# The tail of a scan-and-attention kernel: other engines spread and multiply the last reciprocals, and the last scales, shifts and sums change their order

## The chip, the core and the metric

The kernel runs on one core of a Trainium2 chip. The metric is the device time of one execution in microseconds (us). Engines are named as in the profile: PE is TensorE, DVE is VectorE, ACT is ScalarE, POOL is GpSimd and SP is SyncE.

## What is computed

The input is eight images of 64 channels, 64 x 64. Four directional scans go over them first (each row becomes itself plus relu of a 9-tap convolution of the row before it); the change does not touch them. Then comes linear attention, with four heads of 32 channels, between two group norms:

```python
xn = group_norm(x, gn1_w, gn1_b)
q, k, v = split(conv1x1(xn, w_qkv))            # heads of 32 channels, 4096 positions
q = elu(q) + 1; k = elu(k) + 1
k_sum = k.sum(positions); kv = k^T v           # per head
out = (q @ kv) / (q @ k_sum + 1e-6)
out = group_norm(conv1x1(out, w_out), gn2_w, gn2_b) + x
```

## The kernel before

After the scans the images are in `cols_w`. The attention takes them one after another, b = 0 to 7 (B = 8), through `iteration(b, par, cur, prev, pp)`, which every engine has in a version of its own. Iteration b computes keys, values and queries of image b (`cur`), the denominators, their reciprocals and the first outputs of image b-1 (`prev`), and the second group norm of image b-2 (`pp`). Each engine goes through its own instructions in the order in which they are written; semaphores join the engines.

An image is 4 chunks of 512 columns (128 partitions: two halves of 64 channels). The queries of an image are 8 units of 128 x 512 in `qp`, two to a chunk. To divide by the denominators:

- PE sums them (`denominators`, L586), DVE takes the reciprocals (L901), 128 x 128 for each half m of the units (units 0 to 3, 4 to 7).
- `broadcast(c, m)` on SP writes them to HBM (L320) and reads them back spread over the partitions of a head (L326) into `recip_b`.
- POOL multiplies four units (`normalise_units`, L395) and PE projects two units to one chunk of output (`output`, L597), which ACT copies to SBUF (`collect`, L1142).
- The second group norm: statistics of four chunks on DVE (L912), their aggregate (L906), two matmuls with one column (`group_sums`, L560) with small DVE operations between them, then on POOL a power, a product and a shift (`scale_and_shift`: L399, L403, L407), on ACT scale and shift (`affine`, L1177), on POOL the sum with the scanned image (L424), and SP's stores (L333).

After iteration 7 each engine has a tail, written out by hand. There are two images in it: the last but one (6), of which half is still to be multiplied and projected, and the last (7). In the tail:

- DVE L994/L995 masks the sums of image 7, PE `last_denominators` (L647) gives its denominators for m = 0 and 1, DVE `last_reciprocal` (L982, L986) the reciprocals.
- PE `reciprocals_back(m)` (L659) spreads them into four PSUM banks `back_ps` by 32 small matmuls, with no DMA. DVE `last_normalised(u)` (L990) multiplies a unit by such a bank. Units 4 to 7 use banks that units 0 to 2 must have left (`normed_last`).
- PE `one_before_last(i)` (L666) projects chunks 2 and 3 of image 6, from units that POOL has multiplied, and `last_output(i)` (L673) the chunks of image 7. DVE takes their statistics from PSUM (L1016), ACT copies them out (L1189).
- `group_sums` (L560) comes twice for image 6 (DVE `deviation(5)`, `variance(6)`, L964 to L973) and twice for image 7 (`deviation(7)`, `variance(8)`).
- POOL: `scale_and_shift` of image 6, three quarters of its sum with the scanned image (`residual(q)`, L436), `scale_and_shift` of image 7, the fourth quarter.
- Image 7 is done in two halves of its rows. First half: DVE L1027 (product with the scale, plus the scanned image), then ACT L1200 adds the shift. Second half: ACT L1197 scales and shifts, DVE L1032 adds the scanned image.
- Each half of an image leaves in two stores of 256 KB, one for each half of the partitions. SP issues all four of image 6 and then two of image 7, in this order; ACT issues the other two of image 7 (L1205).

## Time and profile before

| | us |
|---|---|
| median of 3 runs | 705.79 |
| lowest and highest of the 3 | 705.42 and 707.0 |
| the profiled execution | 706.54 |
| span of its trace | 704.7 |
| mean granted TensorE clock | 0.974 |
| PE, DVE, ACT, POOL busy | 636.4, 570.4, 462.6, 140.8 |

The span is measured from the first to the last event of the trace; the profiled execution took 1.8 us more than its span. The scans take about the first 450 us, the eight images the rest, some 27 us each. The tail that the change rewrites is the stretch from about 664 us to the end. A view in order of time gives a start, a duration, the engine, the line and what was written from what; a group of n instructions has xn. Brackets give the idle time before it and what ended it.

### The profile page before, as it was taken

The numbers are of one execution on the slowest core, as the hardware profiler recorded it, in microseconds if no ns is written. First come the engines' busy times: TensorE is split into PE (matmuls) and PEld (weight loads), VectorE is DVE, ScalarE is ACT, GpSimd is POOL, SyncE is SP. The second block draws the span as 40 slices with busy tenths as digits, with TensorE's granted clock in tenths as the row PEclk, the third lists the DMA queues.
The fourth block names the chain that finished last, engine by engine and source line by source line (L and its number), as shares of the span: only waits on it lengthen the run. The fifth ranks groups of instructions, "written<-read, shape, count | busy, mean of one in ns | idle before, by whom it ended". The sixth has DMA issues, their size and how long they took to land.

```text
span 704.7 us, 27312 instructions
## 1 busy us (share of the span) xinstructions
PE 636.4 (90%) x10484; PEld 538.4 (76%) x10484; DVE 570.4 (81%) x1943; ACT 462.6 (66%) x1061; POOL 140.8 (20%) x115
## 2 busy tenths in 40 slices
PE   4999999999999899999999999698888898898960
PEld 4899999898888899999999999556454464554530
DVE  4899998888888798989999999897595686785682
ACT  3555666999999666666666666574666676676531
POOL 0023000000000000000000000000627658549363
PEclk9999999999999999999999999889999999999995
DMA  9999850000000000000000000002342835835756
GB/s 175 203 201 198 166 108 1 1 0 0 0 0 0 1 2 0 0 0 0 1 1 0 0 0 0 0 2 60 71 106 57 171 85 104 178 74 122 159 87 120
DMA packets 63611, 43.27 MB, mean 61 GB/s; under 512 B 42000, under 2 KB 56144, under 8 KB 63568
## 3 DMA queue, kind: packets, MB, share of 16 engines
q1 hardware_dynamic: 60272, 41.89, 30.1%
q10 hardware_dynamic: 3296, 0.82, 0.6%
q8 instruction: 26, 0.43, 0.3%
q14 instruction: 17, 0.14, 0.1%
HBM read 33.39 MB, written 9.31 MB: 61 GB/s over the span
## 4 chain that ended last, share of the span: by engine, by line
DVE 31%; PE 26%; issue 17%; POOL 12%; ACT 7%; DMA 3%; DVEq 1%; ACTq 1%; POOLq 0%; SPq 0%
PE bank L468 20%; DVE scan_rows L735 9%; POOL rows_h L395 9%; DVE parts L721 8%; DVE parts L735 7%; DVE fin L794 3%; ACT cols_w L1077 3%; POOL fin L424 2%; DMA rows_h<-bounce 2%; ACT parts L1061 2%; DVEq L735 1%; PE bank L597 1%; DMA yn<-L_conv_k_td 1%; PE bank L518 1%; PE bank L544 1%
## 5 line engine op out<-in xcount | busy, mean ns | idle before, releaser
L468 PE MATMUL bank<-parts 128*128 128x124 f16 (+2 forms) x7560 | 433.5, 219 | 16.1 <-DVE parts L236 8.7
L468 PEld LDWEIGHTS bank<-parts 128*128 128x128 f16 x7560 | 417.7, 98 | 31.8 <-issue 12.0
L1061 ACT ACTIVATE parts<-parts 128x128 f16<-128x128 f16 x508 | 157.1, 309 | 125.9 <-DVE parts L735 104.3
L721 DVE TENSOR_TENSOR parts<-scan_rows,parts 128x128 f16<-128x128 f32 x508 | 149.4, 294 | 14.2
L735 DVE SCALAR_TENSOR_TENSOR parts<-bank,cols_w 128x128 f16<-128x128 f32 x378 | 109.5, 290 | 19.9 <-PE bank L468 4.7
L735 DVE SCALAR_TENSOR_TENSOR scan_rows<-bank,cols_w 128x128 f32<-128x128 f32 x378 | 105.7, 280 | 0.1
L395 POOL TENSOR_TENSOR rows_h<-rows_h 128x512 f32<-128x512 f32 x56 | 81.9, 1495 | 73.4 <-DMA rows_h<-bounce 73.4
L384 POOL TENSOR_TENSOR scale<-dev,half 128x2 f32<-128x2 f32 (+1 forms) x2 | 2.1, 1038 | 412.0 <-DVE dev L819 412.0
L1077 ACT ACTIVATE cols_w<-scan_rows 64x256 f32 (+1 forms) x128 | 82.7, 646 | 2.3
L861 DVE SCALAR_TENSOR_TENSOR kp<-ex,bank 128x512 f32<-128x512 f32 x64 | 40.8, 679 | 43.4 <-ACT ex L1155 42.4
L1069 ACT ACTIVATE cols_w<-scan_rows 128x256 f32 x126 | 52.5, 417 | 5.7 <-DVE scan_rows L735 0.3
L1163 ACT ACTIVATE ex<-bank,minus_one 128x512 f32<-128x512 f32 x64 | 40.5, 688 | 17.2 <-PE bank L530 16.7
L1155 ACT ACTIVATE ex<-bank,minus_one 128x512 f32<-128x512 f32 x64 | 40.6, 689 | 13.0 <-PE bank L518 13.0
L735 DVE SCALAR_TENSOR_TENSOR parts<-bank,rows_h 128x128 f16<-128x128 f32 x126 | 36.7, 291 | 15.3 <-PE bank L468 7.9
L871 DVE SCALAR_TENSOR_TENSOR rows_h<-ex,bank 128x512 f32<-128x512 f32 x64 | 40.9, 679 | 5.2 <-ACT ex L1163 5.2
L544 PEld LDWEIGHTS bank<-kp,tok 128*64 128x64 f32 x512 | 28.7, 139 | 13.9 <-issue 10.5
L544 PE MATMUL bank<-kp,tok 128*64 128x128 f32 x512 | 35.7, 282 | 1.6 <-DVE kp L861 1.6
L597 PE MATMUL bank<-rows_h,mix 128*64 128x512 f32 x104 | 28.0, 615 | 8.8 <-POOL rows_h L395 8.6
L735 DVE SCALAR_TENSOR_TENSOR scan_rows<-bank,rows_h 128x128 f32<-128x128 f32 x126 | 35.2, 280 | 0.0
L1128 ACT ACTIVATE tok<-bank 128x512 f32<-128x512 f32 x32 | 19.2, 599 | 15.8 <-PE bank L504 15.7
L794 DVE BATCH_NORM_STATS2 fin<-cols_w x96 | 28.7, 299 | 0.0
L1142 ACT ACTIVATE rows_h<-bank 128x512 f32<-128x512 f32 x26 | 15.7, 605 | 19.5 <-PE bank L597 19.4
(133 smaller groups left out, 549.2 us busy)
## 6 DMA issues: line engine op xcount, KB each, us to landing
rows_h<-bounce SPq DMA_DIRECT2D x56, 256.0 KB, 5.0
cols_w<-x SPq DMA_DIRECT2D x12, 896.0 KB, 13.8
out<-fin SPq DMA_DIRECT2D x12, 512.0 KB, 7.7
cols_w<-x SPq DMA_DIRECT2D x6, 640.0 KB, 10.8
cols_w<-x SPq DMA_DIRECT2D x6, 256.0 KB, 7.2
out<-rows_h SPq DMA_DIRECT2D x6, 256.0 KB, 4.7
bounce<-recip SPq DMA_DIRECT2D x14, 64.0 KB, 3.3
out<-rows_h ACTq DMA_DIRECT2D x2, 256.0 KB, 6.5
```

Of the source, the lines that this page charges most:

```text
L395: nc.gpsimd.tensor_tensor(qp[:, 1 - par, u, :], qp[:, 1 - par, u, :], recip_b[:, u, :], ALU.mult).then_inc(normed, 1)
L468: last = nc.tensor.matmul(conv_rows[g][u % SLOTS][:, :, to], w[:, k, d, :], rows_16[:, u % SLOTS, g * GB:(g + 1) * GB, of], start=part_n = ...
L544: nc.tensor.matmul(acc_ps[d * C:(d + 1) * C, 0:P], tok[:, i % 2, n * P + d * C:n * P + (d + 1) * C], kp[:, (2 * i + d) % 4, n * P:(n + 1) ...
L721: nc.vector.tensor_tensor(low[:, slot, gb, :], state[:, slot, gb, :], high[:, slot, gb, :], ALU.subtract).then_inc(low_ready[g], 1)
L735: nc.vector.scalar_tensor_tensor(out=to, in0=conv[g][u % SLOTS][:, 0:GB * J].rearrange("p (b j) -> p b j", b=GB), scalar=0.0, in1=add, op0 ...
L794: nc.vector.bn_stats(stats[:, b, bass.ds(n * 2 + (g - 2), 1), :].rearrange("p o s -> p (o s)"), cols[:, bass.ds(n * -BODY + (W + first), c ...
L861: nc.vector.scalar_tensor_tensor(out=kp[:, m % 4, :], in0=ex[:, m % 2, :], scalar=1.0, in1=key_ps[m % 2][:, :], op0=ALU.min, op1=ALU.max)\
L871: nc.vector.scalar_tensor_tensor(out=qp[:, par, u, :], in0=ex[:, 2 + u % 2, :], scalar=1.0, in1=query_ps[u % 2][:, :], op0=ALU.min, op1=AL ...
L1061: act.activation(high_down[:, slot, gb, :], high[:, slot, gb, :], ACT.Copy, scale=1.0 / LOW_SCALE).then_inc(down_ready[g], 1)
L1069: act.activation(to, state[:, slot, :, :], ACT.Copy).then_inc(saved, 1)
L1077: s = act.activation(dst, state[pw * C:(pw + 1) * C, (u + 1) % SLOTS, :, :], ACT.Copy)
L1155: act.activation(ex[:, m % 2, :], key_ps[m % 2][:, :], ACT.Exp, bias=minus_one[:, :])\
```

## The change

Image 6, the last but one: its second half of reciprocals no longer goes through HBM (`broadcast(B - 2, 1)` and POOL's `normalise_units` are left out in iteration 7). PE spreads them with `reciprocals_back(B - 2, 1, back_before_ps)`, and DVE multiplies units 4 to 7 of image 6 (`normalised_before_last`). The projection of its chunk 1 moves from iteration 7 to the tail.

Image 7, the last: DVE multiplies units 0 to 5. ACT copies the spread reciprocals of units 6 and 7 to `recip_b`, and POOL multiplies them (new semaphores `back_copied`, `normed_late`). The outputs come in the order 0, 1, 3, 2.

The end: POOL computes the scale of image 7 after one quarter of image 6's sum instead of three; its shift is computed by DVE; ACT does image 6's `affine` after two of the four copies of image 7; DVE's last sum no longer waits for ACT's last step.

```diff
+LAST_ORDER = (0, 1, 3, 2)
...
+        back_before_ps = (key_ps[0], key_ps[1], tok_ps, query_ps[0])
...
@@ SyncE @@
-            for m in range(2):
-                broadcast(B - 2, m)
+            broadcast(B - 2, 0)
...
             for h, rows in enumerate(HALVES):
-                sp.wait_ge(last_ready, h + 1)
+                sp.wait_ge(last_ready[h], 1)
                 store(B - 1, rows, fin_tail[:, 1], (0,))
@@ GpSimd @@
-                if prev:
+                if prev and has_next(b, cur):
                     normalise_units(b, par, 1)
...
+            for u in (6, 7):
+                pool.wait_ge(back_copied, u - 5)
+                nc.gpsimd.tensor_tensor(qp[:, 1, u, :], qp[:, 1, u, :], recip_b[:, u, :], ALU.mult)\
+                    .then_inc(normed_late, 1)
             pool.wait_ge(tail_read, 6)
             scale_and_shift(B, 0)
-            for q in range(3):
+            residual(0)
+            pool.wait_ge(tail_read, 8)
+            scale_of_output(B + 1, 1)
+            for q in (1, 2, 3):
                 residual(q)
-            pool.wait_ge(tail_read, 8)
-            scale_and_shift(B + 1, 1)
-            residual(3)
@@ TensorE @@
-                    if i == 3 and prev:
+                    if i == 3 and prev and has_next(b, cur):
...
                         output(b - 1, 1 - par, 1)
...
+            pe.wait_ge(back_loaded, 16)
+            pe.wait_ge(kp_ready, KBANKS * B)
+            pe.wait_ge(tok_ready, 4 * B)
+            pe.wait_ge(qp_ready, UNITS * B - 1)
+            reciprocals_back(B - 2, 1, back_before_ps)
+            pe.wait_ge(acc_read, B)
+            pe.wait_ge(qp_ready, UNITS * B)
+            sums(query_ps[1]).then_inc(tail_done, 1)
             pe.wait_ge(small_read, small_step(B - 1, 5))
+            pe.wait_ge(normed, UNITS * (B - 2) + 4)
+            one_before_last(1)
+            pe.wait_ge(tail_read, 1)
             pe.wait_ge(proj_read, NCHUNK * (B - 2) + 2)
...
+            last_denominators(0)
+            pe.wait_ge(normed_before, 2)
+            one_before_last(2)
+            last_denominators(1)
             pe.wait_ge(tail_read, 2)
             nc.tensor.matmul(small_ps[:, 0:C], kv[:, :], w_o[:, :], start=True, stop=True).then_inc(tail_done, 1)
...
+            pe.wait_ge(normed_before, 4)
             one_before_last(3)
+            reciprocals_back(B - 1, 0, back_ps[0:4])
             pe.wait_ge(normed_last, 3)
             pe.wait_ge(tail_read, 3)
-            reciprocals_back(1)
+            reciprocals_back(B - 1, 1, back_ps[4:8])
...
+            pe.wait_ge(normed_last, 4)
             last_output(1)
-            last_output(2)
+            pe.wait_ge(normed_last, 5)
+            pe.wait_ge(normed_late, 2)
+            last_output(3)
             pe.wait_ge(stat_ready, 2 * B)
             pe.wait_ge(tail_read, 5)
             group_sums(dev2[:, 2:3]).then_inc(tail_done, 1)
-            last_output(3)
+            pe.wait_ge(normed_last, 6)
+            last_output(2)
@@ VectorE @@
+            def normalised_before_last(u):
+                dve.wait_ge(back_done, 1)
+                nc.vector.tensor_tensor(qp[:, 0, u, :], qp[:, 0, u, :], back_before_ps[u - 4][:, :], ALU.mult)\
+                    .then_inc(normed_before, 1)
...
             def tail():
+                stats_before_last(0)
+                for u in (4, 5):
+                    normalised_before_last(u)
                 dve.wait_ge(tail_done, 1)
...
+                for u in (6, 7):
+                    normalised_before_last(u)
+                last_reciprocal(0)
                 stats_before_last(1)
-                for m in range(2):
-                    last_reciprocal(m)
+                last_reciprocal(1)
...
+                for u in (0, 1):
+                    last_normalised(u)
                 stats_before_last(2)
-                for u in range(4):
-                    last_normalised(u)
+                last_normalised(2)
                 stats_before_last(3).then_inc(norm2, 1)
                 aggregate_output(norm2, B - 1)
-                for u in (4, 5):
+                for u in (3, 4):
                     last_normalised(u)
...
-                for u in (6, 7):
-                    last_normalised(u)
+                last_normalised(5)
                 variance(6)
-                for i in range(NCHUNK):
-                    dve.wait_ge(last_out, i + 1)
+                for n, i in enumerate(LAST_ORDER):
+                    dve.wait_ge(last_out, n + 1)
                     nc.vector.bn_stats(stats2[:, i, :], last_ps[i][:, :]).then_inc(last_stated, 1)
...
+                nc.vector.tensor_scalar(shift2[:, 1:2], dev2[:, 3:4], scale2[:, 1:2], norm[:, 3:4], ALU.mult, ALU.add)\
+                    .then_inc(affine_ready, 1)
                 nc.vector.scalar_tensor_tensor(out=fin_tail[:, 1, first, :].rearrange("p j w -> p w j"), in0=mine(first),
...
                 dve.wait_ge(last_affine, 1)
-                dve.wait_ge(last_ready, 1)
@@ ScalarE @@
-                    collect(b - 1, 1 - par, (0, 1))
+                    collect(b - 1, 1 - par, (0,) if isinstance(b, int) and b == B - 1 else (0, 1))
...
-                affine(B - 1, 1, slice(0, J))
-                for i in (2, 3):
+                for i in (1, 2, 3):
                     act.wait_ge(proj_done, NCHUNK * (B - 2) + i + 1)
...
+                    if i == 1:
+                        affine(B - 1, 1, slice(0, J))
+                act.wait_ge(back_done, 3)
+                for u in (6, 7):
+                    act.activation(recip_b[:, u, :], back_ps[u][:, :], ACT.Copy).then_inc(back_copied, 1)
                 act.wait_ge(fin_ready, B - 1)
-                for i in range(NCHUNK):
-                    act.wait_ge(last_stated, i + 1)
+                for n, i in enumerate(LAST_ORDER):
+                    act.wait_ge(last_stated, n + 1)
                     act.activation(proj[:, 1, chunk_of(i)], last_ps[i][:, :], ACT.Copy).then_inc(last_read, 1)
-            for rows in HALVES:
-                affine(B, 0, rows)
+                    if n == 1:
+                        for rows in HALVES:
+                            affine(B, 0, rows)
```

`scale_of_output` is `scale_and_shift` without its last operation. `sums(to)` is `sums()` with the bank given; in the tail it now writes `query_ps[1]` instead of `small_ps`.

PE, from the sums of image 7 to the spreading of its first reciprocals. `kv`, `den_w`, `mix` are weights and `recip` the reciprocals. Before:

```order
L597 MATMUL bank<-rows_h,mix 64x512 [waits normed,proj_read,small_read]
L597 MATMUL bank<-rows_h,mix 64x512
L555 MATMUL bank<-part,acc_s 128x128 [waits acc_read,proj_read,small_read]
L555 MATMUL bank<-part,acc_s 128x128
L557 MATMUL bank<-acc_g,w_v 128x128
L647 MATMUL bank<-rows_h,den_w 32x128 [waits qp_ready,tail_read]
L647 MATMUL bank<-rows_h,den_w 32x128 x31
L686 MATMUL bank<-w_o,kv 128x64 [waits tail_read]
L666 MATMUL bank<-rows_h,mix 64x512 [waits normed]
L666 MATMUL bank<-rows_h,mix 64x512
L659 MATMUL bank<-recip,scan_rows 128x128 [waits recip_ready,kp_ready,back_loaded]
L659 MATMUL bank<-recip,scan_rows 128x128 x15
```

With the change (ahead of these rows stand the 16 small matmuls of L670 for image 6 and the sums L566; the trace counts a float32 matmul twice):

```order
L568 MATMUL bank<-acc_g,w_v 128x128
L676 MATMUL bank<-rows_h,mix 64x512 [waits normed,small_read]
L676 MATMUL bank<-rows_h,mix 64x512
L658 MATMUL bank<-rows_h,den_w 32x128 [waits proj_read,tail_read]
L658 MATMUL bank<-rows_h,den_w 32x128 x15
L676 MATMUL bank<-rows_h,mix 64x512 [waits normed_before]
L676 MATMUL bank<-rows_h,mix 64x512
L658 MATMUL bank<-rows_h,den_w 32x128 x16
L704 MATMUL bank<-w_o,kv 128x64 [waits tail_read]
L676 MATMUL bank<-rows_h,mix 64x512 [waits normed_before]
L676 MATMUL bank<-rows_h,mix 64x512
L670 MATMUL bank<-recip,scan_rows 128x128 [waits recip_ready]
```

The output of chunk 3 of image 6 (the third pair of L676) now stands ahead of the spreading (L670, before L659), and that of chunk 1 (first pair) behind the sums, where L597 stood ahead of them; the pairs of L676 wait for DVE's products (`normed_before`) instead of POOL's.

PE, from the second spreading of image 7 to its last output. Before:

```order
L659 MATMUL bank<-recip,scan_rows 128x128 [waits recip_ready,tail_read,normed_last]
L659 MATMUL bank<-recip,scan_rows 128x128 x15
L673 MATMUL bank<-rows_h,mix_last 64x512 [waits normed_last,proj_read,tail_read]
L673 MATMUL bank<-rows_h,mix_last 64x512
L560 MATMUL bank<-agg,cst 128x1 [waits stat_ready]
L673 MATMUL bank<-rows_h,mix_last 64x512 [waits normed_last,proj_read]
L673 MATMUL bank<-rows_h,mix_last 64x512
L673 MATMUL bank<-rows_h,mix_last 64x512 [waits normed_last]
L673 MATMUL bank<-rows_h,mix_last 64x512
L560 MATMUL bank<-dev,cst 128x1 [waits tail_read,stat_ready]
L673 MATMUL bank<-rows_h,mix_last 64x512 [waits normed_last]
```

With the change:

```order
L670 MATMUL bank<-recip,scan_rows 128x128 [waits recip_ready,tail_read,normed_last]
L670 MATMUL bank<-recip,scan_rows 128x128 x15
L682 MATMUL bank<-rows_h,mix_last 64x512 [waits proj_read,tail_read]
L682 MATMUL bank<-rows_h,mix_last 64x512
L571 MATMUL bank<-agg,cst 128x1 [waits stat_ready]
L682 MATMUL bank<-rows_h,mix_last 64x512 [waits normed_last,proj_read]
L682 MATMUL bank<-rows_h,mix_last 64x512
L682 MATMUL bank<-rows_h,mix_last 64x512 [waits normed_late,normed_last]
L682 MATMUL bank<-rows_h,mix_last 64x512
L571 MATMUL bank<-dev,cst 128x1 [waits tail_read,stat_ready]
L682 MATMUL bank<-rows_h,mix_last 64x512 [waits normed_last]
L682 MATMUL bank<-rows_h,mix_last 64x512
```

The one-column matmul on `dev` now stands behind the output that waits for `normed_late`, POOL's two products.

POOL from the sum of image 5 on. Before:

```order
L424 TENSOR_TENSOR fin<-rows_h,cols_w 128x64x32 [waits stored,affine_done]
L399 TENSOR_TENSOR scale<-dev,half 128x1 [waits tail_read]
L403 TENSOR_SCALAR scale<-scale,norm 128x1 [waits scale_ready]
L407 TENSOR_SCALAR shift<-dev,scale,norm 128x1 [waits scale_ready]
L436 TENSOR_TENSOR rows_h<-rows_h,cols_w 128x64x8 [waits affine_done] x3
L399 TENSOR_TENSOR scale<-dev,half 128x1 [waits tail_read]
L403 TENSOR_SCALAR scale<-scale,norm 128x1 [waits scale_ready]
L407 TENSOR_SCALAR shift<-dev,scale,norm 128x1 [waits scale_ready]
L436 TENSOR_TENSOR rows_h<-rows_h,cols_w 128x64x8 [waits affine_done]
```

With the change:

```order
L431 TENSOR_TENSOR fin<-rows_h,cols_w 128x64x32 [waits stored,affine_done]
L451 TENSOR_TENSOR rows_h<-rows_h 128x512 [waits back_copied] x2
L403 TENSOR_TENSOR scale<-dev,half 128x1 [waits tail_read]
L407 TENSOR_SCALAR scale<-scale,norm 128x1 [waits scale_ready]
L414 TENSOR_SCALAR shift<-dev,scale,norm 128x1 [waits scale_ready]
L443 TENSOR_TENSOR rows_h<-rows_h,cols_w 128x64x8 [waits affine_done]
L403 TENSOR_TENSOR scale<-dev,half 128x1 [waits tail_read]
L407 TENSOR_SCALAR scale<-scale,norm 128x1 [waits scale_ready]
L443 TENSOR_TENSOR rows_h<-rows_h,cols_w 128x64x8 [waits affine_done] x3
```

Two products (L451) are new, ahead of the scale of image 6; the scale of image 7 (second L403, L407) stands behind one quarter of the sums (L443) instead of three, and the shift L414 is gone there.

## Rows read from the trace of the kernel before

**Rows 1.** The chain that ended last, in order of time: start, us, what.

```profile
690.59 1.99 POOLq L81
...
694.99 1.89 DVE rows_h L1032
```

**Rows 2.** PE in order of time, in the tail: start, us, engine, line, what.

```profile
668.59 0.68 PE L555 MATMUL bank<-part,acc_s 128*128 128x128 f32 x4 [1.23 <-ACT acc_s L1134]
...
670.07 1.95 PE L647 MATMUL bank<-rows_h,den_w 128*32 128x128 f32 x64 [0.58 <-DVE kv L995]
...
672.32 1.08 PE L666 MATMUL bank<-rows_h,mix 128*64 128x512 f32 x4
673.33 1.17 PE L659 MATMUL bank<-recip,scan_rows 32*128 32x128 f32 x32
...
676.61 1.17 PE L659 MATMUL bank<-recip,scan_rows 32*128 32x128 f32 x32 [1.09 <-DVE rows_h L990]
...
680.90 0.38 PE L560 MATMUL bank<-dev,cst 128*128 128x1 f32 x2
```

**Rows 3.** DVE in order of time, in the tail.

```profile
669.74 0.28 DVE L995 TENSOR_TENSOR kv<-bank,cst 128x128 f32<-128x128 f32 x1
...
671.54 0.95 DVE L986 RECIPROCAL recip<-den 128x128 f32<-128x128 f32 x1
...
674.69 2.46 DVE L990 TENSOR_TENSOR rows_h<-rows_h,bank 128x512 f32<-128x512 f32 x4
...
681.39 2.48 DVE L1016 BATCH_NORM_STATS2 stats<-bank 128x6 f32<-128x512 f32 x4
...
685.89 0.16 DVE L973 TENSOR_SCALAR dev<-bank 128x1 f32<-128x1 f32 x1 [0.54 <-PE bank L560]
690.51 1.95 DVE L1027 SCALAR_TENSOR_TENSOR rows_h<-rows_h,scale,cols_w 128x1024 f32<-128x1024 f32 x1 [4.46 <-POOL scale L403]
```

**Rows 4.** ACT in order of time: its four copies of image 7.

```profile
682.18 2.33 ACT L1189 ACTIVATE rows_h<-bank 128x512 f32<-128x512 f32 x4 [6.02 <-DVE stats L1016]
```

**Rows 5.** POOL in order of time, in the tail.

```profile
668.64 4.99 POOL L395 TENSOR_TENSOR rows_h<-rows_h 128x512 f32<-128x512 f32 x4 [1.63 <-DMA rows_h<-bounce]
...
685.71 3.68 POOL L436 TENSOR_TENSOR rows_h<-rows_h,cols_w 128x512 f32<-128x512 f32 x3 [2.54 <-ACT rows_h L1177]
...
689.34 0.56 POOL L399 TENSOR_TENSOR scale<-dev,half 128x1 f32<-128x1 f32 x1
690.11 0.28 POOL L403 TENSOR_SCALAR scale<-scale,norm 128x1 f32<-128x1 f32 x1 [0.20 <-POOL scale L399]
690.61 1.97 POOL L407 TENSOR_SCALAR shift<-dev,scale,norm 128x1 f32<-128x1 f32 x1 [0.21 <-POOL scale L403]
```

**Rows 6.** In order of time, 634 to 637 us: POOL beside DVE.

```profile
634.01 2.62 DVE L258 TENSOR_TENSOR parts<-yn,parts 128x2048 f16<-128x2048 f32 x1
634.44 3.32 POOL L395 TENSOR_TENSOR rows_h<-rows_h 128x512 f32<-128x512 f32 x1
...
636.80 0.27 DVE L890 TENSOR_SCALAR dev<-dev,agg 128x1 f32<-128x1 f32 x1
```

**Rows 7.** SP in order of time: the first stores of image 6.

```profile
688.21 1.32 SPq L333 DMA_DIRECT2D out<-rows_h  x2
```

**Rows 8.** Busy by stretch: length, each engine (instructions), granted clock, DMA share, GB/s.

```profile
689.45:692.60 3.15, 0.00 (x0) 0.00 (x0) 1.95 (x1) 0.00 (x0) 2.73 (x4) 0.50 0.96 164
695.05:703.45 8.40, 0.00 (x0) 0.00 (x0) 1.82 (x1) 0.00 (x0) 0.00 (x0) 0.50 0.97 186
```

**Rows 9.** The same view of two stretches, for PE and its clock.

```profile
494.00:498.00 4.00, 1.54 (x34) 1.26 (x34) 2.26 (x4) 3.92 (x7) 2.56 (x3) 0.98 0.13 35
674.00:678.00 4.00, 2.91 (x58) 1.69 (x52) 3.77 (x7) 0.64 (x2) 4.00 (x1) 1.00 0.00 0
```

**Rows 10.** PE in order of time: one form at the lower and at the full clock.

```profile
498.20 1.98 PE L544 MATMUL bank<-kp,tok 128*64 128x128 f32 x16
...
652.15 1.09 PE L544 MATMUL bank<-kp,tok 128*64 128x128 f32 x16
```

More of the change, by code:

```diff
@@ L211, in build @@
         last_stated = sem("last_stated")
-        last_out, last_read, last_sum, last_affine, last_ready = (sem("last_out"), sem("last_read"), sem("last_sum"),
-                                                                  sem("last_affine"), sem("last_ready"))
+        last_out, last_read, last_sum, last_affine = (sem("last_out"), sem("last_read"), sem("last_sum"),
+                                                      sem("last_affine"))
+        normed_before, back_copied, normed_late = sem("normed_before"), sem("back_copied"), sem("normed_late")
+        last_ready = [sem(f"last_ready{h}") for h in range(2)]
         proj_done, proj_read = sem("proj_done"), sem("proj_read")
@@ L404, in scale_and_shift @@
                                         ALU.mult).then_inc(scale_ready, 1)
+            def scale_and_shift(b, par):
+                scale_of_output(b, par)
                 at_least(pool, scale_ready, 2 * b)
@@ L551, in gather, with sums @@
                 last.then_inc(acc_used, 1)
-            def sums():
+            def sums(to):
                 for d in range(2):
-                    nc.tensor.matmul(small_ps[:, 0:P], acc_s[:, d * P:(d + 1) * P], part[:, :],
+                    nc.tensor.matmul(to[:, 0:P], acc_s[:, d * P:(d + 1) * P], part[:, :],
                                      start=d == 0, stop=d == 1)
-                return nc.tensor.matmul(small_ps[:, P:2 * P], w_v[:, :], acc_g[:, :], start=True, stop=True)
+                return nc.tensor.matmul(to[:, P:2 * P], w_v[:, :], acc_g[:, :], start=True, stop=True)
             def group_sums(v):
@@ L571, in small @@
                     at_least(pe, acc_read, b)
-                    last = sums()
+                    last = sums(small_ps)
                 if n == 2:
@@ L658, in reciprocals_back @@
                         here = slice(DH * u, DH * (u + 1))
-                        last = nc.tensor.matmul(back_ps[4 * m + u][:, s * SUB:(s + 1) * SUB], back_to_heads[here, s, :],
+                        last = nc.tensor.matmul(to[u][:, s * SUB:(s + 1) * SUB], back_to_heads[here, s, :],
                                                 recip[here, m, :], start=True, stop=True)
@@ L663, in one_before_last @@
             def one_before_last(i):
-                pe.wait_ge(normed, UNITS * (B - 2) + 2 * i + 2)
                 for d in range(2):
-                    last = nc.tensor.matmul((out_ps, tok_ps)[i - 2][d * C:(d + 1) * C, :], mix[:, :], qp[:, 0, 2 * i + d, :],
-                                            start=True, stop=True)
+                    last = nc.tensor.matmul((small_ps, out_ps, tok_ps)[i - 1][d * C:(d + 1) * C, :], mix[:, :],
+                                            qp[:, 0, 2 * i + d, :], start=True, stop=True)
                 last.then_inc(proj_done, 1)
             def last_output(i):
-                pe.wait_ge(normed_last, 2 * i + 2)
                 for d in range(2):
@@ L1030, in tail @@
                 dve.wait_ge(last_affine, 1)
-                dve.wait_ge(last_ready, 1)
                 nc.vector.tensor_tensor(fin_tail[:, 1, second, :].rearrange("p j w -> p w j"), mine(second),
-                                        cols[:, :, B - 1, second], ALU.add).then_inc(last_ready, 1)
+                                        cols[:, :, B - 1, second], ALU.add).then_inc(last_ready[1], 1)
             for i in range(NCHUNK):
```

34 lines of the change are left out of this document (12 added, 22 removed).

## The prediction

> **What bounds the kernel now.** The change leaves all before 664 us as it is, so I read the tail: the chain that ended last, then each engine in order of time, then busy time by stretch. PE runs almost without a gap from the denominators of image 7 (670.07) to its first spreading (673.33), waits 1.09 us for DVE's third product before the second (676.61), and is through at 682.3 [rows 2]. DVE takes the four statistics of image 7 from 681.39 to 683.87, and the last number that its scale needs is there at 686.05 (685.89 + 0.16) [rows 3]. But POOL starts that scale at 689.34, since three quarters of image 6's sum (685.71 to 689.39) stand ahead of it; the scale is ready at 690.39, and the shift takes 1.97 us where DVE's sum lies over it [rows 5]. The chain ends with that shift and DVE's last sum, done at 696.88 [rows 1]. The stores end the span: the DMA engines are full (share 0.97) from 695.05 to 703.45 with six of the eight stores of 256 KB, 8.40 / 6 = 1.40 us each, and the span ends 1.25 us behind them, at 704.7 [rows 8]. So there are two things to gain: 3.3 us of POOL's order, and what the start of the stores allows. Times below are on this trace's scale.
>
> **To the first spreading: 0.96 us later.** PE gets 16 small matmuls more for image 6, a spreading of 1.17 us, behind which the next group can start after some 1.10 [rows 2]. They start at 666.3, where the output of chunk 1 stood, and fill PE's old wait of 1.23 us for ACT's copy [rows 2]; ACT comes earlier itself, for it no longer copies chunk 1 first. The sums end at 668.3, the output of chunk 1 at 669.3. DVE multiplies units 4 and 5 from 667.5, at 0.61 us each (2.46 / 4 [rows 3]), and masks the sums by 669.3, before which `kv` was ready at 670.02 [rows 3]. What counts is another wait: the denominators need the bank that chunk 1 is in, and ACT must copy it out, 0.6 us (2.33 / 4 is 0.58 [rows 4]). They start at 670.03, as before. Behind them PE has, as before, two denominator groups, a small product and the output of chunk 2, which took from 670.07 to 673.33, and, new ahead of the spreading, the output of chunk 3, 1.01 us from start to start (673.33 - 672.32) [rows 2]. PE has no gap there, so the first spreading starts at 674.29 instead of 673.33. Its reciprocal (671.4 to 672.35 by the 0.95 us of its row [rows 3]) is not late. The four products of POOL that go (4.99 us, begun at 668.64 on a DMA's arrival [rows 5]) were ready when PE wanted them, so their removal gains nothing here; it lets POOL and the stores of images 4 and 5 start earlier, which nobody waits for.
>
> **To the statistics: 2.6 us later.** The spreading ends at 675.46. DVE makes products 0 and 1, then the statistics of chunk 2 (0.62 us), which it did before the products in a gap until now, then product 2: it is done at 678.0, where it was at 676.56. So the second spreading starts at 678.05, 1.44 us later than in its row [rows 2]. It ends at 679.22. ACT copies two banks (0.60 and 0.58), POOL multiplies unit 6 from 679.93 and unit 7 until 682.43 (1.25 each, 4.99 / 4 [rows 5]). PE has output 0, the sums and output 1 beside that and is free at 681.5; it waits 1 us for POOL, starts the output of chunk 3 at 682.5 and the one-column matmul behind it at 683.5 (0.38 long [rows 2]). **DVE waits for this matmul** (`variance(6)`), and all four statistics of image 7 are queued behind it, though two chunks have been there since 681.5. They run from 684.0 to 686.5 (2.48 us) instead of 681.39 to 683.87 [rows 3]: 2.6 us later. The two products that DVE gives away (1.2 us) would have fitted into its wait.
>
> **To the scale: 0.55 us earlier.** From the last statistics to `variance(8)` it took 686.05 - 683.87 = 2.2 us [rows 3]: now 688.7. POOL starts image 6's scale and shift at 684.2, does one quarter of the sum until 688.5 (ACT's first half of `affine` comes right behind its second copy), and is free. Power and product take 0.56 + 0.20 + 0.28 with a start lag of 0.1 [rows 5]: ready at 689.85 instead of 690.39. Of the 3.3 us that stood in POOL's queue, 2.6 went to the late statistics.
>
> **The end: 1.1 us later.** POOL and DVE cannot work side by side on two operands in SBUF: one product of POOL, begun at 634.44, takes 3.32 us instead of 1.25 while DVE's L258 (634.01 to 636.63) lies over it [rows 6]; the shift of 0.33 us at other places took 1.97 beside L1027 [rows 5]. Now three quarters of image 6's sum (1.23 each, 3.68 / 3) and DVE's two sums (1.95 and 1.89) all start after 689.9 and take turns: 3.7 + 3.85 = 7.55 us, so the last quarter ends at 697.4, whoever goes first. Until now it ended at 693.8. DVE's own last sum is done by 695 to 696.3, before 696.88. SP issues in order, so four stores, the second half of image 6 and SP's two of image 7, go only after 697.4. From the first issue to the first traffic it took 689.45 - 688.21 = 1.24 us [rows 7, 8]; four stores at 1.40 to 1.57 us (3.15 / 2, two alone) take 5.6 to 6.3; the tail of the span is 1.25 [rows 8]. I take 1.5 us a store: 697.4 + 1.24 + 6.0 + 1.25 = 705.9, against 704.7. From the last statistics on that is 19.4 us. The shift on DVE is at 0.27 us (L890, one column, beside a running product of POOL [rows 6]), and hidden: DVE's sum waits for POOL's quarter anyway. Bounds: nothing (it runs inside that wait) to 0.3.
>
> **TensorE's clock: 0.7 us.** PE would stand still from 675.5 to 678.05, and be busy some 1.2 us of 674.3 to 678. Before 498 it was busy 1.54 of 4 us and fell to the lower level (1.2 GHz): 16 matmuls took 1.98 us right after, 1.09 at 2.4 GHz. In 674 to 678 it has been busy 2.91 of 4 so far, and the clock held [rows 9, 10]. By these two rows a fall at 678 to 680 is more likely than not. It doubles the second spreading and the output behind it, about 1.0 and 0.9 us; POOL's way and PE's share them, so the path loses 0.5 to 1.0. I take 0.7.
>
> **Sum.** 1.2 + 0.7 = 1.9 us longer. The profiled execution took 706.54, the median is 705.79, 0.75 lower; I add to the median: 707.7 us.
>
> **Rivals.**
>
> *The clock holds* (0.23). Then 1.2 us remain, or 0.9 to 1.4 by the bounds on a store: 707.0. For it: one stretch of 4 us tells little of what the chip looks at, and where PE's pause lies in it.
>
> *The statistics are not late, and POOL's new order pays: faster* (0.12). If POOL's two products come in time or PE's gap is shorter than I find, the last statistics end at 683.9 as before, and 19.4 us later is 703.3: 1.4 us less, 704.4. The point that decides is the end of the last statistics: before 684.0 the kernel is faster by more than 0.2%. Against it: it takes 2.6 us that each engine's order accounts for.
>
> *The lower clock stays through the outputs* (0.08). Outputs 0, 1 and 3 take 0.9 more each, the spreading 1.0, the sums 0.3: 4.0 less the 1 us for which PE now waits, 3.0 us on top of 707.0: 710.0.
>
> *The shift on DVE waits for POOL* (0.05). If it holds off until POOL's quarter ends and another quarter slips between it and the sum, only its own length is added to the turns: 0.3, 708.0. The Trainium skill, SBUF — State Buffer, Who interferes with whom, says that a `tensor_scalar` from SBUF to SBUF can take the pair of ports shared with GpSimd, and that the second of the two then blocks wholly. By that the shift would wait up to a quarter's 1.2 us; the row of L890 shows no such wait for this form.
>
> The rest (0.52) is the forecast, 706.8 to 708.7.
>
> **Chances.** 0.2% is 1.4 us, about what a measurement of this kernel can tell from no change; slower begins at 707.2. The forecast's case lies above it with two thirds, the held clock with a quarter, the last two wholly: 0.35 + 0.06 + 0.13 = 0.54. Faster: 0.10 of the rival's 0.12. Same: 0.36. The range is 705.0 to 709.2; outside are most of the faster case, the long fall of the clock, and little of the others.
>
> **What would show it.** Right: the first spreading of image 7 at about 674.3 and the second near 678; a gap of 2.5 us on PE between them; DVE idle before `variance(6)` for over 2 us, its releaser PE; statistics from 684; POOL's last three quarters and DVE's two sums stretched against each other until 697; four stores behind that. Wrong: statistics that end before 685, or quarters of 1.25 us beside DVE's sums, which would let the stores of image 6 go by 694 (they would still need 8 x 1.40 us from 692.4 on, and end at 704.9).

## The result, and the profile after

| | before | changed |
|---|---|---|
| median, us | 706.93 (8 runs, 705.08 to 707.82) | 708.65 (8 runs, 707.85 to 710.53) |
| ratio | 1 | 1.0029, interval 1.0017 to 1.0042 |
| span of the trace, us | 704.7 | 706.6 |
| PE, DVE, ACT, POOL busy, us | 636.4, 570.4, 462.6, 140.8 | 639.4, 572.8, 463.7, 139.4 |

The change makes the kernel 0.29% slower, by 1.7 us of the medians. The prediction said 1.9 us and, added to a median of 705.79 for the kernel before, 707.7; the kernel before came out at 706.93 here, and the changed one at 708.65. The times of both kernels scatter by 2.7 us, and so does the moment at which the tail begins, although nothing ahead of it was changed. So the traces are compared from PE's last group of matmuls on the keys (L548 before, L559 now), which starts at 665.70 before and at 664.96 now. The row of before:

```profile
665.70 0.64 PE L548 MATMUL bank<-kp,ones 128*32 128x256 f32 x8
```

PE in order of time, the tail of the changed kernel, against [rows 2]:

```profile
664.96 0.64 PE L559 MATMUL bank<-kp,ones 128*32 128x256 f32 x8
665.53 1.17 PE L670 MATMUL bank<-recip,scan_rows 32*128 32x128 f32 x32
...
669.36 1.08 PE L658 MATMUL bank<-rows_h,den_w 128*32 128x128 f32 x32 [0.79 <-ACT rows_h L1214]
...
672.76 1.08 PE L676 MATMUL bank<-rows_h,mix 128*64 128x512 f32 x4
673.77 1.17 PE L670 MATMUL bank<-recip,scan_rows 32*128 32x128 f32 x32
677.54 2.09 PE L670 MATMUL bank<-recip,scan_rows 32*128 32x128 f32 x32 [2.60 <-DVE rows_h L1015]
679.56 1.98 PE L682 MATMUL bank<-rows_h,mix_last 128*64 128x512 f32 x4
681.47 0.59 PE L571 MATMUL bank<-agg,cst 128*128 128x1 f32 x2
681.98 2.86 PE L682 MATMUL bank<-rows_h,mix_last 128*64 128x512 f32 x8
684.77 0.38 PE L571 MATMUL bank<-dev,cst 128*128 128x1 f32 x2
```

The reader is to see three things: the spreading for image 6 at 665.53, where an output stood; the gap of 2.60 us ahead of the second spreading of image 7; and that spreading at 2.09 us instead of 1.17, the output behind it at 1.98 instead of 1.08.

DVE in order of time, against [rows 3]:

```profile
675.01 1.28 DVE L1015 TENSOR_TENSOR rows_h<-rows_h,bank 128x512 f32<-128x512 f32 x2 [1.12 <-PE bank L670]
...
685.19 0.16 DVE L992 TENSOR_SCALAR dev<-bank 128x1 f32<-128x1 f32 x1 [1.90 <-PE bank L571]
685.27 2.48 DVE L1045 BATCH_NORM_STATS2 stats<-bank 128x6 f32<-128x512 f32 x4
...
689.71 0.16 DVE L992 TENSOR_SCALAR dev<-bank 128x1 f32<-128x1 f32 x1 [0.48 <-PE bank L571]
691.10 0.27 DVE L1056 TENSOR_SCALAR shift<-dev,scale,norm 128x1 f32<-128x1 f32 x1 [1.24 <-POOL scale L407]
691.29 2.68 DVE L1058 SCALAR_TENSOR_TENSOR rows_h<-rows_h,scale,cols_w 128x1024 f32<-128x1024 f32 x1
693.82 2.91 DVE L1062 TENSOR_TENSOR rows_h<-rows_h,cols_w 128x1024 f32<-128x1024 f32 x1
```

The statistics of image 7 start right behind `variance(6)`, for which DVE stood still 1.90 us with PE as the releaser. The two sums, 1.95 and 1.89 us before, take 2.68 and 2.91.

POOL in order of time, against [rows 5]:

```profile
680.37 2.49 POOL L451 TENSOR_TENSOR rows_h<-rows_h 128x512 f32<-128x512 f32 x2 [4.52 <-ACT rows_h L1220]
...
688.40 1.26 POOL L443 TENSOR_TENSOR rows_h<-rows_h,cols_w 128x512 f32<-128x512 f32 x1 [1.36 <-ACT rows_h L1207]
...
690.71 0.28 POOL L407 TENSOR_SCALAR scale<-scale,norm 128x1 f32<-128x1 f32 x1 [0.21 <-POOL scale L403]
690.96 6.78 POOL L443 TENSOR_TENSOR rows_h<-rows_h,cols_w 128x512 f32<-128x512 f32 x3
```

The last three quarters take 6.78 us; three of them took 3.68 alone. The chain that ended last now ends in them:

```profile
690.71 0.28 POOL scale L407
690.99 1.22 POOLq L83
692.21 5.52 POOL rows_h L443 x2
```

Busy time by stretch, against [rows 8, 9] (length, each engine, granted clock, DMA share, GB/s):

```profile
674.00:678.00 4.00, 1.40 (x40) 1.21 (x40) 2.99 (x5) 0.48 (x1) 1.85 (x1) 0.88 0.23 35
676.50:677.00 0.50, 0.00 (x0) 0.00 (x0) 0.50 (x2) 0.00 (x0) 0.00 (x0) 1.00 0.00 0
677.50:683.50 6.00, 5.96 (x42) 3.10 (x44) 3.17 (x8) 1.08 (x2) 2.49 (x2) 0.50 0.98 162
684.00:688.00 4.00, 2.17 (x10) 0.49 (x6) 2.67 (x6) 1.95 (x3) 1.20 (x3) 1.00 0.00 0
```

```profile
693.55:705.30 11.75, 0.00 (x0) 0.00 (x0) 3.17 (x2) 1.15 (x1) 4.18 (x2) 0.50 0.99 177
```

The granted clock falls in the first stretch, inside PE's gap (1.00 until 677.00), stays at 0.50, which is 1.2 GHz, from 677.50 to 683.50, and is 1.00 again from 684.00. In the stretch of the stores the DMA engines are full from the first store to the last: before, they paused between two stretches of stores.

**The tail in three pieces.** K is the start of the last group on the keys, S the start of the first spreading of image 7, L the end of the last statistics, E the end of the span. Each is worked out from the rows of that kernel's trace.

| kernel | K to S | S to L | L to E | K to E |
|---|---|---|---|---|
| before | 7.63 | 10.54 | 20.83 | 39.0 |
| changed | 8.81 | 13.98 | 18.85 | 41.6 |
| e1 | 7.62 | 10.55 | 18.8 | 36.9 |
| e2 | 8.81 | 12.74 | 21.2 | 42.8 |
| e3 | 8.81 | 12.31 | 18.7 | 39.9 |
| e4 | 8.81 | 11.72 | 18.7 | 39.3 |
| e5 | 8.81 | 12.94 | 17.8 | 39.5 |
| e6 | 8.82 | 12.70 | 18.6 | 40.2 |
| e8 | 8.81 | 10.24 | 19.0 | 38.1 |
| e9 | 7.63 | 9.70 | 18.9 | 36.2 |
| e10 | 7.80 | 12.32 | 18.8 | 38.9 |
| e11 | 7.63 | 9.70 | 17.55 | 34.9 |
| e12 | 7.80 | 10.24 | 17.5 | 35.6 |

Against before, the changed kernel has +1.18, +3.44 and -1.98: 2.6 us more in the tail. Its trace entered the tail 0.74 us earlier, hence 1.9 in the span.

### The profile page after: what moved, and what is told of

It is laid out like the page before. It is cut to its first block, busy times and chain, and to the rows that moved or that the text cites. A ratio compares the mean times of both kernels' runs of the same rounds, so it can differ in the third digit from the quotient of the medians.

```text
span 706.6 us, 27368 instructions
## 1 busy us (share of the span) xinstructions
PE 639.4 (90%) x10516; PEld 540.0 (76%) x10516; DVE 572.8 (81%) x1946; ACT 463.7 (66%) x1063; POOL 139.4 (20%) x112
## 4 chain that ended last, share of the span: by engine, by line
DVE 31%; PE 27%; issue 17%; POOL 12%; ACT 6%; DMA 3%; DVEq 1%; ACTq 1%; SPq 0%; POOLq 0%
PE bank L479 20%; DVE scan_rows L754 9%; POOL rows_h L399 9%; DVE parts L740 7%; DVE parts L754 7%; DVE fin L813 3%; ACT cols_w L1107 3%; POOL fin L431 2%; DMA rows_h<-bounce 2%; ACT parts L1091 2%; DVEq L754 1%; POOL rows_h L443 1%; PE bank L608 1%; DMA yn<-L_conv_k_td 1%; PE bank L682 1%
## 5 line engine op out<-in xcount | busy, mean ns | idle before, releaser
L740 DVE TENSOR_TENSOR parts<-scan_rows,parts 128x128 f16<-128x128 f32 x508 | 149.1, 294 | 14.2
L399 POOL TENSOR_TENSOR rows_h<-rows_h 128x512 f32<-128x512 f32 x52 | 76.7, 1507 | 72.1 <-DMA rows_h<-bounce 72.1
L555 PEld LDWEIGHTS bank<-kp,tok 128*64 128x64 f32 x512 | 28.5, 139 | 13.8 <-issue 10.8
L555 PE MATMUL bank<-kp,tok 128*64 128x128 f32 x512 | 35.4, 281 | 1.6 <-DVE kp L880 1.6
L431 POOL TENSOR_TENSOR fin<-rows_h,cols_w 128x2048 f32<-128x2048 f32 x6 | 27.5, 4585 | 4.7 <-ACT rows_h L1207 4.7
```

The lines of the kernel that those rows point to most:

```text
L399: nc.gpsimd.tensor_tensor(qp[:, 1 - par, u, :], qp[:, 1 - par, u, :], recip_b[:, u, :], ALU.mult).then_inc(normed, 1)
L431: nc.gpsimd.tensor_tensor(fin[:, :, :].rearrange("p j w -> p w j"), proj[:, par, :].rearrange("p (w j) -> p w j", j=J), cols[:, :, bass.ds ...
L555: nc.tensor.matmul(acc_ps[d * C:(d + 1) * C, 0:P], tok[:, i % 2, n * P + d * C:n * P + (d + 1) * C], kp[:, (2 * i + d) % 4, n * P:(n + 1) ...
L740: nc.vector.tensor_tensor(low[:, slot, gb, :], state[:, slot, gb, :], high[:, slot, gb, :], ALU.subtract).then_inc(low_ready[g], 1)
```

## Experiments

The kernels were timed in three groups, 6 to 12 runs of each, and each group on one chip together with the kernel before. The medians of before were 706.99 us for e1 to e4, 706.75 for e5 to e9 and 707.07 for e10 to e12. So kernels of different groups are compared by their ratios to before. A trace is one execution, and the times of a kernel scatter by more than most of the effects looked for.

| kernel | median, us | ratio to before, interval |
|---|---|---|
| e1 new end alone | 704.76 | 0.9965, 0.995 to 0.9979 |
| e2 old end | 710.72 | 1.0054, 1.0038 to 1.0071 |
| e3 PE busy in the gap | 707.16 | 1.0011, 1.0 to 1.0023 |
| e4 sums first | 708.06 | 1.0019, 1.0006 to 1.0032 |
| e5 last image's stores first | 707.01 | 0.9997, 0.9978 to 1.0015 |
| e6 DVE multiplies all units | 707.22 | 1.0, 0.9984 to 1.0016 |
| e8 = e3 + e4 | 705.84 | 0.9975, 0.9958 to 0.9992 |
| e9 = e1 + POOL's two products | 703.97 | 0.996, 0.9944 to 0.9976 |
| e10 output 3 behind | 706.63 | 0.9989, 0.9975 to 1.0004 |
| e11 = e9 + order of stores | 703.11 | 0.9942, 0.9921 to 0.9962 |
| e12 all four mended | 703.3 | 0.9942, 0.992 to 0.9963 |

### e1 and e2: the two ends, each with the other front

e1 is the kernel before with the new end (the lines on POOL, DVE and ACT):

```diff
-            for q in range(3):
-                residual(q)
-            pool.wait_ge(tail_read, 8)
-            scale_and_shift(B + 1, 1)
-            residual(3)
+            residual(0)
+            pool.wait_ge(tail_read, 8)
+            scale_of_output(B + 1, 1)
+            for q in (1, 2, 3):
+                residual(q)
...
+                nc.vector.tensor_scalar(shift2[:, 1:2], dev2[:, 3:4], scale2[:, 1:2], norm[:, 3:4], ALU.mult, ALU.add)\
+                    .then_inc(affine_ready, 1)
...
-                dve.wait_ge(last_ready, 1)
...
-                for rows in HALVES:
-                    affine(B, 0, rows)
+                    if i == 1:
+                        for rows in HALVES:
+                            affine(B, 0, rows)
```

> The kernel before with the new end alone: POOL computes the scale of image 7 after one quarter of image 6's sum, DVE computes the shift, ACT does image 6's affine after two copies, DVE's last sum does not wait for ACT's last step. Nothing ahead of the statistics changes. Theory of the late statistics: the last statistics end about 683.9 on the scale of the trace before, the span ends 18.9 to 19.4 us behind them, 1.4 to 1.9 us shorter than before (ratio 0.9973 to 0.998). Rival, that the new end itself costs the time (POOL and DVE take turns, the last quarter and four stores come late): 1 us longer than before (1.0015).

e2 is the reverse edit, in the changed kernel.

> The changed kernel with the old end (three quarters of image 6's sum, then scale and shift of image 7 on POOL). Theory of the late statistics: from the last statistics to the end of the span it is 20.8 us as in the trace before, so the span is 1.9 us longer than the changed kernel's and 3.5 to 4 us longer than before's (ratio 1.005). Rival, that the new end costs the time: as fast as the kernel before, or the changed kernel less 1 us (1.000 to 1.0015).

DVE and POOL of e1, in order of time:

```profile
682.36 2.48 DVE L1020 BATCH_NORM_STATS2 stats<-bank 128x6 f32<-128x512 f32 x4
...
688.46 2.67 DVE L1033 SCALAR_TENSOR_TENSOR rows_h<-rows_h,scale,cols_w 128x1024 f32<-128x1024 f32 x1
690.99 2.90 DVE L1037 TENSOR_TENSOR rows_h<-rows_h,cols_w 128x1024 f32<-128x1024 f32 x1
```

```profile
687.88 0.28 POOL L404 TENSOR_SCALAR scale<-scale,norm 128x1 f32<-128x1 f32 x1 [0.21 <-POOL scale L400]
688.12 6.77 POOL L440 TENSOR_TENSOR rows_h<-rows_h,cols_w 128x512 f32<-128x512 f32 x3
```

The new end alone gives 0.35%, 2.5 us of 707, and its trace 2.07 us between L and E; taking it out of the changed kernel costs 2.4 us there. POOL and DVE take the same turns in e1 (6.77 us for three quarters), so the turns are no reason for the slowdown: the rival that the new end costs the time falls. All that is lost in the traces lies ahead of L.

### e3: is it the clock?

```diff
             reciprocals_back(B - 1, 0, back_ps[0:4])
+            pe.wait_ge(proj_read, NCHUNK * (B - 2) + 3)
+            for _ in range(10):
+                nc.tensor.matmul(out_ps[:, :], first_rows[:, :], row_of_ones[:, :], start=True, stop=True)
```

> The changed kernel with ten extra f16 matmuls of 512 columns on PE, about 2.2 us, in the gap of 3 us between the two spreadings of image 7; they write a bank that nobody reads before it is written again. Theory of the clock: the granted clock stays 1.00 from 674 to 684, the second spreading takes 1.17 us instead of 2.09 and the output behind it 1.08 instead of 1.98, PE then waits about 1 us for POOL, and the last statistics come 1.5 to 1.8 us earlier relative to the second spreading: ratio to the changed kernel 0.9975, to the kernel before 1.0005. Rival, that the waits for POOL take the place of the slow matmuls: less than 0.5 us gained, ratio 1.002 to 1.003.

PE of e3, in order of time:

```profile
676.67 2.33 PE L710 MATMUL bank<-row_of_ones,first_rows 128*128 128x512 f16 x10
679.33 1.17 PE L670 MATMUL bank<-recip,scan_rows 32*128 32x128 f32 x32 [0.33 <-DVE rows_h L1018]
680.44 1.08 PE L682 MATMUL bank<-rows_h,mix_last 128*64 128x512 f32 x4
...
683.88 1.08 PE L682 MATMUL bank<-rows_h,mix_last 128*64 128x512 f32 x4 [1.05 <-POOL rows_h L451]
```

With work that nobody needs the tail gets shorter: S to L is 12.31 us instead of 13.98, 1.67 us less. The granted clock of e3 stays at 1.00:

```profile
674.00:684.00 10.00, 8.62 (x104) 4.20 (x94) 7.01 (x16) 1.68 (x3) 6.14 (x3) 1.00 0.51 83
```

The second spreading takes 1.17 again, and the wait of 1 us for POOL that the prediction had worked out comes to light (1.05). The time goes from 1.0029 to 1.0011, 1.3 us; those two intervals overlap by a little, so it is the rows that show it, and the times only agree. All five kernels with the whole gap of 2.60 us (changed, e2, e4, e5, e6) fell to the lower clock in their traces, with second spreadings of 1.61 to 2.09 us; the four with a gap of 1.59 or less (e3, e8, e10, e12) kept 1.17 or 1.18. The fall does not always come at the same moment: 3.3 us behind S in the changed kernel, 4.1 in e5 and 4.3 in e2. With PE's order alike, S to L was 13.98, 12.94 (e5) and 12.74 (e2), so against e3's 12.31 its price was 1.7, 0.6 and 0.4 us.

### e4, e6 and e8: the queue behind POOL's products

```diff
-LAST_ORDER = (0, 1, 3, 2)
+LAST_ORDER = (0, 1, 2, 3)
...
-            pe.wait_ge(normed_last, 5)
-            pe.wait_ge(normed_late, 2)
-            last_output(3)
             pe.wait_ge(stat_ready, 2 * B)
             pe.wait_ge(tail_read, 5)
             group_sums(dev2[:, 2:3]).then_inc(tail_done, 1)
             pe.wait_ge(normed_last, 6)
             last_output(2)
+            pe.wait_ge(normed_late, 2)
+            last_output(3)
```

> The changed kernel with PE's order behind output 1 rewritten: the one-column matmul on which variance(6) waits first, then output 2 and then output 3, which waits for POOL's two products; statistics in the order 0, 1, 2, 3. Theory of the queue: DVE no longer stands still before variance(6); the last statistics end 1.9 us earlier where the clock holds, 2.4 us where it falls as in the changed kernel's trace, relative to the second spreading; ratio to the kernel before 0.999 to 1.0005. Rival, that PE is the bound through the outputs (slow clock) and DVE's queue does not count: less than 0.8 us gained, ratio 1.002 or more.

> e3 and e4 together: PE busy in the gap, and the one-column matmul and output 2 ahead of output 3. If the clock and the queue are two costs that add up: last statistics 10.5 to 11 us behind the start of the first spreading (kernel before: 10.5), as they are in the kernel before; what is left against it is the 1.2 us ahead of the spreading, less the 2.0 us that the new end gives: ratio 0.9985 to 0.9995. Rival, that they overlap: no better than e3 (1.0011).

DVE of e4, in order of time:

```profile
683.15 0.16 DVE L991 TENSOR_SCALAR dev<-bank 128x1 f32<-128x1 f32 x1
683.22 2.54 DVE L1044 BATCH_NORM_STATS2 stats<-bank 128x6 f32<-128x512 f32 x4
```

PE and DVE of e8:

```profile
673.95 1.17 PE L670 MATMUL bank<-recip,scan_rows 32*128 32x128 f32 x32
677.72 1.17 PE L670 MATMUL bank<-recip,scan_rows 32*128 32x128 f32 x32 [0.34 <-DVE rows_h L1017]
681.65 2.54 DVE L1047 BATCH_NORM_STATS2 stats<-bank 128x6 f32<-128x512 f32 x4
```

The wait ahead of `variance(6)` is gone in both. S to L falls by 2.26 us in e4's trace; with the clock held in both, from 12.31 (e3) to 10.24 (e8), 2.07 us. The two costs add up, nearly: 1.67 and 2.26 alone, 3.74 together, and e8's 10.24 is shorter than before's 10.54. In time e4 missed what was expected of it: it gained only 0.1%, less than its trace, and its interval overlaps with the changed kernel's. Its trace is of the fastest of its 12 runs (706.33 us). e8 gained 0.54% and is clear of the changed kernel. How much e4 gives without e3 stays open.

e6 leaves out POOL's products and ACT's two copies and lets DVE do units 6 and 7 ahead of `variance(6)`:

> The changed kernel with no products on POOL: DVE multiplies units 6 and 7 too, ACT does not copy their banks, and PE's order behind output 1 is as in e4 (one-column matmul, output 2, output 3). Theory of the queue: what POOL's part costs is the order behind it, so this is near e4: DVE has 1.2 us more ahead of variance(6), the last statistics end 12 to 13 us behind the start of the first spreading (e4: 11.7, the changed kernel: 14.0), ratio to the kernel before 1.002 to 1.003. Rival, that POOL's way (two copies, two products) is what makes the statistics late: 11 us or less, ratio 1.001 or less.

S to L is 12.70 us, against 11.72 in e4, both with the lower clock: POOL's two products, in an order that lets DVE go on, are worth 1 us in these two traces. The clock fell later in e6 than in e4 (4.3 and 3.6 us behind S), so it does not explain that e6 is longer. The time (1.0, interval 0.9984 to 1.0016) is lower than expected of the trace and can't separate e6 from e4.

### e10: the output ahead of the first spreading

```diff
             pe.wait_ge(normed_before, 4)
-            one_before_last(3)
             reciprocals_back(B - 1, 0, back_ps[0:4])
+            one_before_last(3)
```

> The changed kernel with the output of image 6's chunk 3 behind the first spreading of image 7 instead of ahead of it, as it stood before the change. Theory: the first spreading starts 1.0 us earlier (8.8 us instead of 9.8 behind the start of PE's last group on the keys), the output fills 1 us of PE's gap, and the span behind that group is 1.0 us shorter than the changed kernel's 41.6, or up to 2.5 us where the clock then holds: ratio to the kernel before 0.9995 to 1.0015. Rival, that DVE's statistics of chunk 3 wait for the later output and give it back: no gain, 1.0025 or more.

```profile
672.40 1.17 PE L670 MATMUL bank<-recip,scan_rows 32*128 32x128 f32 x32
673.50 1.08 PE L676 MATMUL bank<-rows_h,mix 128*64 128x512 f32 x4
676.17 1.18 PE L670 MATMUL bank<-recip,scan_rows 32*128 32x128 f32 x32 [1.59 <-DVE rows_h L1015]
```

K to S falls from 8.81 to 7.80, the gap from 2.60 to 1.59, and the clock holds: S to L is 12.32, e3's value to 0.01 us, without any extra work. Moving one line took away both costs, 0.4% of the time (1.0029 to 0.9989, the intervals apart). DVE did not wait for the later output. (The 9.8 and 8.8 us of the expectation are counted from the group of matmuls ahead of K, L555; from there it was 9.79 and is 8.77.)

### e5: the order of the stores

```diff
+            first, second = HALVES
+            sp.wait_ge(fin_ready, B)
+            store(B - 2, first, fin_tail[:, 0])
             for h, rows in enumerate(HALVES):
-                sp.wait_ge(fin_ready, B + h)
-                store(B - 2, rows, fin_tail[:, 0])
-            for h, rows in enumerate(HALVES):
                 sp.wait_ge(last_ready[h], 1)
                 store(B - 1, rows, fin_tail[:, 1], (0,))
+            sp.wait_ge(fin_ready, B + 1)
+            store(B - 2, second, fin_tail[:, 0])
```

> The changed kernel with SP's two stores of image 7 ahead of its two stores of image 6's second half. Theory of the last quarter (as in the prediction: four stores can only go when POOL's last quarter is done): two stores move ahead of it, and the span behind the last statistics shrinks from 18.9 us by 1 to 2 us (ratio to the kernel before 1.000 to 1.0015). Rival, that the DMA engines are busy without a gap from the first store on, so that only the start of that stream and eight stores count: no gain, span still 18.5 to 19 us behind the last statistics, ratio 1.0029 as the changed kernel.

DMA of e5 from first to last traffic, by stretch:

```profile
694.65:705.30 10.65, 0.00 (x0) 0.00 (x0) 3.18 (x2) 1.15 (x1) 4.19 (x2) 0.50 1.01 194
```

L to E is 17.8, 1.1 us less, as the theory of the last quarter expected. The rival had its premise right and its conclusion wrong: the engines were full in the changed kernel too (0.99), but the same eight stores take 10.65 us in this order and 11.75 in the other, at 194 GB/s against 177. The wait for the last quarter, over at 697.74, left no pause in the changed kernel's stream. What differs is the rate, low in the first half of the stream and higher behind it:

```profile
693.55:699.50 5.95, 0.00 (x0) 0.00 (x0) 3.17 (x2) 1.15 (x1) 4.18 (x2) 0.50 0.98 163
700.00:705.30 5.30, 0.00 (x0) 0.00 (x0) 0.00 (x0) 0.00 (x0) 0.00 (x0) 0.50 1.01 196
```

Whether an earlier last quarter, with the stores in their old order, would raise the rate as well was not tried. From the first store's issue to the end of the span it is 14.2 to 14.4 us in the changed kernel, e1, e8 and e9, and 13.0 to 13.1 in e5, e11 and e12, the three with this order. The time of e5 says 0.9997, more than its trace; the interval reaches to 1.0015.

### e9, e11 and e12: put together

e9 is e1 with POOL's two products and the order of e4; e11 adds e5's order of stores. What e9 adds to e1, on POOL, PE and DVE:

```diff
+            for u in (6, 7):
+                pool.wait_ge(back_copied, u - 5)
+                nc.gpsimd.tensor_tensor(qp[:, 1, u, :], qp[:, 1, u, :], recip_b[:, u, :], ALU.mult)\
+                    .then_inc(normed_late, 1)
...
             last_output(1)
-            last_output(2)
             pe.wait_ge(stat_ready, 2 * B)
             pe.wait_ge(tail_read, 5)
             group_sums(dev2[:, 2:3]).then_inc(tail_done, 1)
+            last_output(2)
             last_output(3)
...
-                for u in (6, 7):
-                    last_normalised(u)
                 variance(6)
```

> The kernel before (image 6 by DMA and POOL as it was, no outputs ahead of the first spreading) with the new end and, from the change, only POOL's two products of image 7, with PE's one-column matmul ahead of output 2 and 3. Theory: POOL's products are done 7.7 us behind the start of the first spreading, output 3 8.8, the last statistics 9.5 to 9.8 (e1: 10.55), so 0.8 to 1 us faster than e1: ratio to the kernel before 0.995. Rival, that POOL's way costs more than DVE's two products: 10.5 us or more, ratio 0.9965 or more.

> e9 with the order of stores of e5. If two queues with stores under way move more bytes a microsecond than one, as e5's trace shows against the changed kernel's: 0.8 to 1.2 us less than e9, ratio to the kernel before 0.9945. Rival, that e5's gain was chance: as e9, 0.996.

e12 is the changed kernel with the orders of e4, e5 and e10 and five extra matmuls in PE's gap:

> The changed kernel with e4's order, e5's stores, e10's order and five extra matmuls in what is left of PE's gap. If the four costs are separate: span behind PE's last group on the keys 36 us (before 39.0, changed 41.6), ratio 0.9955 to 0.9965, which says that image 6's spreading by PE costs nothing by itself beyond its order. Rival, that they overlap: no better than e8, 0.9975 or more.

DVE's statistics of e9:

```profile
680.75 0.16 DVE L984 TENSOR_SCALAR dev<-bank 128x1 f32<-128x1 f32 x1 [0.72 <-PE bank L569]
680.82 2.50 DVE L1025 BATCH_NORM_STATS2 stats<-bank 128x6 f32<-128x512 f32 x4
```

e9 has S to L at 9.70, 0.85 less than e1; its time does not tell it from e1 (0.996 and 0.9965). e11 has e9's first two pieces to 0.01 us and 1.3 us less from L to E (17.55, e9 18.9), so the gain of the order of the stores came a second time. e11 and e12 are the fastest, 0.58% below before, 4.1 us, and 0.9% below the changed kernel. With the orders mended and PE kept busy, image 6's spreading by PE costs 0.7 us of tail against e11 (35.6 and 34.9) and nothing that the times can tell. It gains nothing over the old way by DMA and POOL either.

## Why the prediction held, step by step

- **To the first spreading, 0.96 later: 1.18 by the trace.** The denominators start 4.40 us behind K, before 4.37: ACT's copy is the wait, as worked out (0.79 <-ACT). Behind them it is 4.41 us instead of 3.26; the output of chunk 3 is 1.01 of it, and two denominator groups apart take 1.01 each from start to start where together they took 0.95 each. e10 shows the cost of the output alone: 1.01.
- **To the second spreading.** Worked out 3.76 us behind the first; measured 3.77, and 3.28 before.
- **To the statistics, with the clock held.** Worked out as 8.45 us from the second spreading to L (678.05 to 686.5); e3 has 8.54, with its wait of 1.05 for POOL. That DVE's queue behind `variance(6)` makes it is shown by e8.
- **The clock, 0.7: the term that was mis-sized.** It took 1.67 in the changed kernel's trace and 0.4 to 1.7 over the traces. The prediction had the fall at 678 to 680 and counted the spreading and one output; it came at 677, and the lower clock lasted until 683.5 at least, so that the sums and about half of the next two outputs fell under it too. That PE's way would then take the place of the wait for POOL was right: the wait is not in the changed kernel's trace.
- **To the scale.** Worked out 3.35 behind L, measured 3.24.
- **The turns of POOL and DVE, 7.55: measured 6.78** (690.96 to 697.74). The sums took 2.68 and 2.91 us, and three quarters and two sums, 3.68 and 3.84 alone, overlapped by 0.7. DVE's first sum had to wait for POOL's quarter and POOL for DVE, as the prediction says.
- **The four stores behind the last quarter.** Measured 8.86 from its end to E (worked out 8.5). The size was near. The picture, of four stores that start late and the rest done, was not what the trace shows: the DMA engines were full from the first store on, and the stream of eight stores, 11.75 us, set the end. What of its length is owed to the late start of four stores is open (e5). With the turns shorter than worked out, L to E came to 18.85 instead of 19.4.
- **The shift on DVE.** 0.27 us beside POOL's quarter that had begun at 690.96: it did not wait. The rule of the Trainium skill, SBUF — State Buffer, Who interferes with whom, that a `tensor_scalar` between SBUF operands can be held by GpSimd's instruction, did not show for this form of one column.
- **The sum.** 1.9 us were forecast, 1.2 without the clock; the trace has 1.9 in the span and 2.6 in the tail, the medians 1.7. That the span agrees to 0.1 us is luck: in the tail the part ahead of L came 1.3 us longer than worked out (4.6 against 3.3), mostly the clock, and the part behind it 0.55 shorter, and the tail happened to begin 0.74 us early in this execution. That the medians lie below the tail's 2.6 would fit a clock that costs less in most executions, as it did in e2 and e5; no run shows this. The rival on the other side had its point at the last statistics: e1 puts them back, and the kernel is faster, by 2.1 us in the tail where 1.4 were worked out.
- **Slips in the working.** The end is headed 1.1 us later, but its own sum, 705.9 against 704.7, gives the 1.2 that is used. The bounds of the rival in which the clock holds, 0.9 to 1.4, are 0.8 to 1.5 by stores of 1.40 and 1.57 us. Neither changes the forecast. Of the signs, DVE stood idle 1.90 us before `variance(6)` instead of over 2.

## What to carry to other kernels

A wait is paid by all that stands behind it in its engine's order: here the engine that waited for a helper's two products held a one-column matmul, and that held four statistics of another engine. When a change moves work from a transfer to TensorE, look at the pauses that it opens there as well as at the work: one output moved back behind the spreading took away 1 us of path and cut the pause in which the clock had fallen from 2.60 to 1.59 us, and there the clock held. And a change of two parts can hide a gain: its new end was worth 2 us, its new front cost 4.6.

## What the runs showed of the hardware that was not expected

- The DMA engines' busy share does not tell how fast they move: at shares of 0.99 and 1.01 the same eight stores took 11.75 and 10.65 us (177 and 194 GB/s). In the faster order the stores of the two halves of the partitions go out from SP and ACT side by side, and by the kernel's order more stores can be under way at once; that either is the reason was not tried by itself.
- Sums of two operands in SBUF on DVE and on POOL hold each other up, but not wholly: 6.78 us for what takes 7.5 one after the other. By an estimate from these numbers, each of the four changes between the engines overlaps by 0.2 us.
- With the same order of matmuls the clock does not fall at the same moment: in three traces it came 3.3, 4.1 and 4.3 us behind the start of the first spreading, and cost 1.7, 0.6 and 0.4 us.
